# Embedding lookups, pairwise products and a small tower on one core: products by whole batches, lookups' high halves first, and the last block's first layer taken batch by batch

## The reference

```python
e = jnp.stack([tbl_f[ids[:, f]] for f in range(32)], axis=1)      # 512 x 32 x 256
z = jnp.einsum('bnd,bmd->bnm', e, e)[:, iu, ju]                    # 496 products i < j of each sample
h = jnp.concatenate([z, dense_ctx], axis=1)                        # 512 x 512
h = jnp.maximum(h @ W_top1 + b_top1, 0.0)                          # 512 x 512
h = jnp.maximum(h @ W_top2 + b_top2, 0.0)                          # 512 x 256
y = h @ W_top3                                                     # 512 x 1
```

## Time and profile before

| | |
|---|---|
| median of 3 runs | 164.88 us (163.91 to 168.86) |
| the profiled execution | 164.76 us, of which the span is 163.0 us |
| PE busy | 147.7 us, 91% of the span |
| PE weight loads | 132.3 us |
| DVE, ACT, POOL busy | 81.0, 78.3, 102.7 us |
| mean granted TensorE clock | 0.958 |

### The profile page before, as it was taken

How to read it: one execution, slowest core, us unless ns; L and a number is a source line. 1 busy time by engine, 2 the same in 40 slices (tenths; PEclk the granted TensorE clock), 3 DMA queues, 4 the chain that set the end, 5 groups by cost and what they waited for, 6 DMA issues and landing times.

```text
span 163.0 us, 6485 instructions
## 1 busy us (share of the span) xinstructions
PE 147.7 (91%) x2872; PEld 132.3 (81%) x2872; DVE 81.0 (50%) x212; ACT 78.3 (48%) x180; POOL 102.7 (63%) x110
## 2 busy tenths in 40 slices
PE   6996999999979969849985999999999999949994
PEld 6874888888878959839874989998898898949992
DVE  0798686766278597509500518207606605555000
ACT  3354848576686495607321723625426505363112
POOL 1677777777777777777777777777777777000000
PEclk9999999999999999965997899999999999986999
DMA  4899787868787889994443334333433343100000
GB/s 135 280 339 356 235 262 225 257 225 253 223 229 265 218 232 261 388 368 143 111 117 105 99 109 120 106 103 107 119 107 101 109 119 108 37 0 4 0 6 1
DMA packets 12926, 26.79 MB, mean 164 GB/s; under 512 B 3105, under 2 KB 3809, under 8 KB 12898
## 3 DMA queue, kind: packets, MB, share of 16 engines
q0 software_dynamic: 4992, 13.64, 29.3%
q1 hardware_dynamic: 7762, 12.47, 23.2%
q10 hardware_dynamic: 144, 0.26, 0.5%
HBM read 26.36 MB, written 0.00 MB: 162 GB/s over the span
## 4 chain that ended last, share of the span: by engine, by line
PE 81%; DMA 6%; issue 5%; ACT 4%; POOL 2%; DVE 0%
PE bank L505 24%; PE bank L553 16%; PE xt_ps L523 16%; PE bank L560 15%; PE bank L585 6%; DMA rows<-table,row_ids 4%; PE xt_ps L560 3%; ACT pairs L433 2%; DMA first_sb<-first_ids 2%; POOL rows L311 2%; PE bank L593 1%; ACT xt L416 1%; ACT high L403 1%; ACT kept L411 0%; DVE h L390 0%
## 5 line engine op out<-in xcount | busy, mean ns | idle before, releaser
L311 POOL DMA_INDIRECT rows<-table,row_ids x104 | 102.0, 981 | 34.8 <-issue 29.6
L416 ACT COPY xt<-xt_ps 128x512 f32<-128x512 f32 (+1 forms) x42 | 22.8, 559 | 45.1 <-PE xt_ps L523 44.8
L505 PE MATMUL bank<-one_hot,high 128*128 128x512 f32 (+1 forms) x128 | 35.2, 356 | 1.6 <-ACT kept L411 1.3
L553 PE MATMUL bank<-xt 128*32 128x32 f32 x2048 | 29.1, 203 | 8.3 <-issue 5.8
L553 PEld LDWEIGHTS bank<-xt 128*32 128x32 f32 x2048 | 24.0, 113 | 14.0 <-issue 8.5
L505 PE MATMUL bank<-one_hot,low 128*128 128x512 f32 (+1 forms) x128 | 33.5, 345 | 0.0
L342 DVE COPY xt<-xt_ps 128x512 f32<-128x512 f32 (+1 forms) x14 | 9.2, 654 | 44.4 <-PE xt_ps L523 44.4
L523 PE MATMUL xt_ps<-ident,rows 128*128 128x128 f32 x208 | 29.3, 290 | 1.5 <-DMA rows<-table,row_ids 1.5
L331 DVE TENSOR_SCALAR one_hot<-small_ids_sb,first_sb 128x512 fp32r<-128x512 int32 (+1 forms) x64 | 25.7, 427 | 7.8 <-PE bank L505 7.5
L523 PEld LDWEIGHTS xt_ps<-ident,rows 128*128 128x128 f32 x208 | 24.5, 147 | 3.8 <-DMA rows<-table,row_ids 2.0
L359 DVE COPY pairs<-bank 32x112 f32<-32x112 f32 (+3 forms) x88 | 23.5, 267 | 6.7 <-PE bank L553 5.7
(11 more groups left out here) (23 smaller groups left out, 39.6 us busy)
## 6 DMA issues: line engine op xcount, KB each, us to landing
small_sb<-small_tables SPq DMA_DIRECT2D x32, 256.0 KB, 4.3
w_sb<-w SPq DMA_DIRECT2D x8, 256.0 KB
rows<-table,row_ids POOLq DMA_INDIRECT x104, 3.8
small_ids_sb<-small_ids SPq DMA_DIRECT2D x3, 256.0 KB, 6.3
small_ids_sb<-small_ids SPq DMA_DIRECT2D x4, 128.0 KB, 4.3
w_sb<-w SPq DMA_DIRECT2D x1, 512.0 KB
small_ids_sb<-small_ids ACTq DMA_DIRECT2D x1, 256.0 KB, 3.5
ids_sb<-ids SPq DMA_DIRECT2D x1, 100.0 KB, 3.5
```

Source lines behind the costliest of these rows:

```text
L311: nc.gpsimd.indirect_dma_start(rows[:, i % ROWS, :], None, table, bass.IndirectOffsetOnAxis(ap=row_ids[:, i:i + 1], axis=0)).then_inc(gath ...
L416: nc.scalar.copy(*fill_parts(f)).then_inc(xt_act, 1)
L505: last = nc.tensor.matmul(banks[FOUND_BANKS[k][d]][:, of], part[:, k % TABLES, c, d * P:(d + 1) * P], one_hot[:, i % ONE_HOTS, of], start= ...
L553: done = nc.tensor.matmul(dots_ps[bank][Q * s:Q * (s + 1), u, g, :], x, x, start=(c == 0), stop=(c == DC - 1))
```

## The change

- `dots` are ordered by whole batches: each round has both halves of its batch in one run. The remaining 16 twos stand in rounds 0 to 3, two ahead of the batch and two behind it, instead of in rounds 0 to 5. Layer 1 of block 0 starts in round 5.
- `look_up` takes the four `high` products of its two chunks first, then the four `low` ones, and waits for `low` only there.
- The early fills come by threes (after twos 5, 8, 10, 12) and two after two 14. Warm-up has 9 products.
- A block's samples are numbered batch by batch, so that the 32 samples of a batch lie together in `pairs`. `b_top1` becomes a row of W1 against a row of ones in the dense part, so that a block's first relu is one ACT instruction of 128x512.
- In the last block layer 1 is turned round (`flip`): for each batch, 32 products with 32 samples as weights and 128 columns of W1 moving, four of them side by side in the four strips of PSUM partitions, accumulated over 8. The result (`flip_ps`) is copied to `flipped`, transposed by PE (`turn`), and copied with relu to `h1`. The last batch's six fetches are in four fills (2, 2, 1, 1). `h1` has two buffers.
- DVE moves three of the four strips of products from the second pair of batches on (before: two until the fourth pair), and only one of the first pair.

```diff
-WARM_UP = 12
+WARM_UP = 9
-FILLS_BEHIND = {2: (0, 1), 4: (2, 3), 6: (4, 5), 8: (6, 7), 10: (8, 9), 12: (10, 11), 14: (12, 13)}
+FILLS_BEHIND = {5: (0, 1, 2), 8: (3, 4, 5), 10: (6, 7, 8), 12: (9, 10, 11), 14: (12, 13)}
-LEAD_DOTS = [[0], [2], [4], [6], [8], [10], [13], [15], [17], [19], [21], [23], [25], [27, 28]]
-TRAIL_DOTS = [[1], [3], [5], [7], [9], [11, 12], [14], [16], [18], [20], [22], [24], [26], [29]]
+LEAD_DOTS = [[2 * n, 2 * n + 1] for n in range(6)] + [[2 * n, 2 * n + 1] for n in range(7, 15)]
+TRAIL_DOTS = [[]] * 5 + [[12, 13]] + [[]] * 8
-LEAD_TWOS = [3, 1, 2, 3, 2, 2] + [0] * (ROUNDS - 6)
-TRAIL_TWOS = [0, 2, 1, 0, 0, 0] + [0] * (ROUNDS - 6)
+LEAD_TWOS = [2, 2, 2, 2] + [0] * (ROUNDS - 4)
+TRAIL_TWOS = [2, 2, 2, 2] + [0] * (ROUNDS - 4)
-LAYER1_IN = {6: (0, [0, 1, 2, 3]), 7: (0, [4, 5, 6, 7]), 8: (1, [0, 1]), 9: (1, [2, 3, 4]),
+LAYER1_IN = {5: (0, [0, 1, 2]), 6: (0, [3, 4, 5]), 7: (0, [6, 7]), 8: (1, [0, 1]), 9: (1, [2, 3, 4]),
...
         def dve_quads(v):
-            return range(2 if v < 3 else 3)
+            return range(1 if v == 0 else 3)
...
             def look_up(two):
+                for part in (high, low):
+                    for i in range(2 * two, 2 * two + 2):
+                        if part is high:
+                            pe.wait_ge(one_hot_ready, i + 1)
+                        if i % 2 == 0:
+                            pe.wait_ge(high_ready if part is high else low_ready, two + 1)
...
+            def flip(m):
+                b = NB - 1
+                moved = UNIT * b + max(m, 1)
+                pe.wait_ge(moved_dve, moved)
+                pe.wait_ge(moved_act, moved)
...
+                for j in range(JJ):
+                    for q in range(QUADS):
+                        done = nc.tensor.matmul(flip_ps[m][Q * q:Q * (q + 1), :],
+                                                pairs[:, b % 2, j, m * SAMPLES:(m + 1) * SAMPLES],
+                                                w1_sb[:, j, q * P:(q + 1) * P], start=(j == 0), stop=(j == JJ - 1))
+                done.then_inc(flip_done, 1)
+            def turn(m):
...
+                nc.tensor.transpose(turn_ps[m], flipped[:, m, :], ident[:]).then_inc(turned, 1)
...
                 for f in fills_in(r):
+                    if f == NF - 2:
+                        flip(0)
+                        layer2_of(NB - 2)
+                        turn(0)
                     fill(f)
+            flip(1)
             for half in (2 * NM - 2, 2 * NM - 1):
                 dots(half)
-            layer2_of(b - 1)
...
+            flip(2)
+            flip(3)
+            layer3(NB - 2, l3_ps)
+            for m in range(1, BATCHES):
+                turn(m)
...
+            for n in range(N2):
+                for k in range(N1):
+                    layer2(NB - 1, n, k, last_l2_ps)
+            layer3(NB - 1, last_l3_ps)
```

More of the change, by code:

```diff
@@ L26 @@
 GATHERS = [(N_FIELDS - n) // PER_GATHER for n in LOOKED_UP]
-FILLS = [(n + 1) // 2 for n in GATHERS]
+FILLS = [[2] * (n // 2) + [1] * (n % 2) for n in GATHERS]
+LAST_FILLS = [2] * (GATHERS[1] // 2 - 1) + [1, 1]
 BLOCK = 128
@@ L62, with build_tower @@
 MOVES_IN = {2: 0, 4: 1, 6: 2, 7: 3, 9: 4, 11: 5, 13: 6}
-def build_tower(nc, table, first_ids, ids, small_tables, small_ids, dense, w1, b1, w2, b2, w3, out):
+def build_tower(nc, table, first_ids, ids, small_tables, small_ids, dense, w1, w2, b2, w3, out):
     D = table.shape[1]
@@ L76, in build_tower @@
     NG = sum(GATHERS) * HALF_BATCHES
-    NF = sum(FILLS) * HALF_BATCHES
+    NF = sum(len(fills) for fills in FILLS) * HALF_BATCHES + 1
     assert DC == 2 and KR == P and N_FIELDS == Q and NM == 2 * HALF_BATCHES
-    assert sum(TWOS_IN) == TWOS - FIRST_TWOS and NF == EARLY + ROUNDS * ROUND_FILLS
+    assert sum(TWOS_IN) == TWOS - FIRST_TWOS and NF == EARLY + ROUNDS * ROUND_FILLS + 1
     with ExitStack() as ctx:
@@ L132, in build_tower @@
         no_pairs_zeroed = sem("no_pairs_zeroed")
-        dense_in = sem("dense_in")
+        dense_in = [sem(f"dense_in{n}") for n in range(2)]
         weights_in = sem("weights_in")
@@ L162, in half_of, with fills_of @@
             return n // HALF_BATCHES
+        def fills_of(n):
+            return FILLS[half_of(n)] if n < NM - 1 else LAST_FILLS
         def first_fill(n):
-            return sum(FILLS[half_of(m)] for m in range(n))
+            return sum(len(fills_of(m)) for m in range(n))
         def batch_fill(f):
@@ L175, in fill_gathers @@
             n, u = batch_fill(f)
-            first = sum(GATHERS[half_of(m)] for m in range(n))
-            return range(first + 2 * u, first + min(2 * u + 2, GATHERS[half_of(n)]))
+            first = sum(GATHERS[half_of(m)] for m in range(n)) + sum(fills_of(n)[:u])
+            return range(first, first + fills_of(n)[u])
         def by_dve(f):
-            return f >= EARLY and f % 3 == 0
+            return f >= EARLY and f % 3 == 0 or f == NF - 1
         def moved_fills(f):
@@ L227, in fills_in @@
         def fills_in(r):
-            return range(EARLY + r * ROUND_FILLS, EARLY + (r + 1) * ROUND_FILLS)
+            return range(EARLY + r * ROUND_FILLS, EARLY + (r + 1) * ROUND_FILLS + (r == ROUNDS - 1))
         def dots_place(n):
@@ L492, in look_up @@
             def look_up(two):
-                for i in range(2 * two, 2 * two + 2):
-                    k, c = divmod(i, CHUNKS)
-                    pe.wait_ge(one_hot_ready, i + 1)
-                    if i % 2 == 0:
-                        pe.wait_ge(high_ready, two + 1)
-                        pe.wait_ge(low_ready, two + 1)
-                    of = looked_up_for(k)
-                    for part in (high, low):
+                k = 2 * two // CHUNKS
+                of = looked_up_for(k)
+                for part in (high, low):
+                    for i in range(2 * two, 2 * two + 2):
+                        c = i % CHUNKS
+                        if part is high:
+                            pe.wait_ge(one_hot_ready, i + 1)
+                        if i % 2 == 0:
+                            pe.wait_ge(high_ready if part is high else low_ready, two + 1)
                         for d in range(DC):
@@ L508, in look_up @@
                                 start=(c == 0 and part is high), stop=(c == CHUNKS - 1 and part is low))
-                    last.then_inc(chunk_used, 1)
+                        if part is low:
+                            last.then_inc(chunk_used, 1)
             def fill(f):
@@ L693 @@
     w1[0, 0:dense.shape[1], 0] = W1[len(iu):]
+    w1[0, dense.shape[1], 0] = a["b_top1"]
     arrays = {
@@ L700 @@
         "small_ids": ids_m[:, :, looked_up].reshape(B, most).T[None],
-        "dense": dense.T,
+        "dense": np.concatenate([dense.T, np.ones((1, B), dense.dtype)]),
         "w1": w1.reshape(P, JJ, H1),
-        "b1": a["b_top1"].reshape(-1, P).T,
         "w2": a["W_top2"].reshape(H1 // P, P, -1).transpose(1, 0, 2),
```

133 lines of the change are left out of this document (80 added, 53 removed).

## The result

The changed kernel takes 178.92 us (median of 4 runs, 174.76 to 182.56), the kernel before 164.39 (median of 4): ratio 1.072, 95% interval 1.052 to 1.093. It is slower. The ratio takes of each kernel only the runs within 1.5% of its fastest, so it is lower than that of the medians, 1.088. The profiled execution took 177.12 us with a span of 175.2, the one before 164.76 with 163.0, so 12.2 us of span are to be explained.

The account below looks back on a forecast made before the run. Two close bounds were taken: PE's own work and the fetches it follows. From 164.76 us, first tables -1.0, rounds -0.8 and the end -2.2 gave 160.8 us; the 8-in-10 range was 158.5 to 166.

Parts of the forecast that it names:

- The rounds, waits added: New PE waits in the rounds: +0.9 for `xt` ahead of batch 0, +0.3 in round 2, +6.6 code, +2.1 half clock.
- `kept` in round 2: In round 2 ACT's copy of the third table stands behind 12 product copies and four `high` casts: about +0.3 us.
- The same step, code: PE waits in the rounds for 256-instruction blocks of its program, more and shorter than before: +6.6 us (3 to 11).
- The price: Time a code block needs to come: about 5.2 us while tables load, 4.2 in the rest, 2.9 behind long products.
- Half clock: Loss in the rounds from the clock halving behind waits, taken as half of before: +2.1 us (0 to 5).
- Up to the end of the first tables: Start through the first four tables: fills by threes start earlier, but fetch 24 caps the gain; -1.0 us.
- The flips: Last block's turned layer 1, 64 matmuls of 128 columns each: four side by side, 1.8 us a flip.
- rival B: Flips less than four side by side, 2.25 to 2.9 us each: 162.6 to 165.2 us; chance 0.2, one by one 0.02.
- The end: From the end of round 13's layer 1 to the span's end: 22.0 us before, 19.8 now, -2.2.
- C: Slower: every round's run of 256 meets a block border and pays the full price: 172 us; chance 0.08.
- A: Code waits at low prices, no half clock, landings on time, PE held by fetches: 159.3 to 160.0 us; chance 0.2.
- D: Products' order gives nothing: code waits return at 9 to 10 us, half clock at 4: 164 us; chance 0.15.

## Why the prediction was wrong

**Step that failed: "The rounds, waits added."** It names three waits: `xt` ahead of batch 0, `kept` in round 2, and code. It has none for the fill that each whole batch reads. The profile of before had the row that shows the need, ACT's copies of fills at 559 ns each, and I asked only for batch 0 what stands between a copy and its product. Eight more batches have nothing there. Forecast 0, measured 5.3 us. I even booked the fills' new place (they "now follow layer 1 and not products") as a gain of 0.8.

```profile
L416 ACT COPY xt<-xt_ps 128x512 f32<-128x512 f32 (+1 forms) x42 | 22.8, 559 | 45.1 <-PE xt_ps L523 44.8
```

**The same step, code.** Forecast 6.6 us in eight places, by blocks that take 2.9 to 5.2 us from border to arrival. Measured in all 10.9 (8.0+2.1+0.8), of which 8.1 behind round 6's fills, where I had 1.0 (batches 8 and 11). Batch 3 came out as forecast (1.45 for 1.6), batches 0, 4 and 7 without a wait, batch 5 at half (0.54 for 1.1); batches 8, 9 and 12 waited 1.85, 1.94 and 2.18, where I had 0.3 for the first and nothing for the others, and the layers behind batches 11 and 14 waited 1.31 and 0.79, where I had 0.7 and nothing. The price was the wrong kind of number. A block's time from border to arrival isn't a property of the block: of the five in the quiet part, two had packets that started only 6.3 and 5.5 us behind their border. My working had slips too, of 0.5 us together: by the prices that I name, the terms of batches 3, 4, 5 and 8 are 1.7, 0.6, 1.3 and 0.6, and batch 7's 0.9 follows from none of them. That the blocks are of 256 and that the dense runs meet them was right: the waits in the quiet part end at PE records 3265, 3521, 4289, 4545 and 5313, all multiples of 256 apart.

**Half clock.** Forecast +2.1, as half of before. Measured were four stretches of 3.41 us, near waits of 1.45, 1.85, 1.94 and 2.05. Against the same instructions at full clock each cost about 1.6 us (lookups 1.05 for 0.64, layer 1 3.51 for 1.95), 6.5 together by this estimate. And none came behind the longest code wait, 2.18 at 137.92. The borderline I drew by the length of one stop, between 1.3 and 2.08, isn't there.

**Up to the end of the first tables, -1.0.** Measured +0.2 (fills at 41.23, before at 41.00). Fetch 20 made PE wait 1.80 at 37.30, and that took what fills by threes had won; I had only looked at fetch 24. In round 2 came another wait for rows, of 2.05, for which the forecast had nothing but 0.7 much later.

**Right.** The wait of 0.9 for `xt L424` (0.85). The flips: 64 matmuls in 1.88 us (156.65 to 158.53), against 1.8 forecast, so rival B is off and the estimate of 2.25 from the Trainium skill's "TensorE: Matmul & The Clock Gate" (Measured speedup vs the span model) is too long for them. The wait for code near flip 3 (0.83, forecast 0.7). No wait ahead of the last products. The end: counted as in the forecast, from the end of round 13's layer 1, it took 22.0 us before and 19.5 after, -2.5 against -2.2 forecast. From the start of the fills it is -1.8; the rest is the half batch that stood between that layer and the fills.

**Together.** Copies 5.3, code 4.3, half clock 4.4, the first tables 1.2 and the wait for rows in round 2 some 1.3 over their terms, less 0.3 each for `kept` and the end, make 15.9 of the 16.3 us by which the profiled execution missed 160.8.

**The rivals.** C came nearest (172) for a wrong reason: it put the loss on density, and density with the fills ahead costs nothing that can be measured (0.995). It had 0.08. A and D were both within the mechanism that fell. In the Trainium skill's "Runtime: NRT & Kernel Launch" (Instruction fetch mechanics) the fetch is hidden; neither trace agrees, with 5.8 us of waits for code before and 10.9 after.

## What to carry over

When work is merged into one longer run, ask of its first instruction what it reads and who wrote that last: two short runs with something between them hide a copy that one long run doesn't. A short wait ahead of a dense run can cost more than its length: here 4.7 us of such waits went, seven of the eight, and 13 us of time with them, since the code waits behind them went too. Moving producers ahead of other work only helps while their inputs are there: where PE had come close to the fetches, the fills that were put first waited 7.6 us for them.

## What the hardware showed that I had not expected

- A code packet (16 KB) takes 0.9 to 1.4 us in the changed kernel, and a PE that waits for it resumes 1.3 to 1.5 us after its end (109.76 to 111.22; 136.51 to 137.92), while tables load too (73.08 to 74.54). The rest of a block's time is the time until the packet starts.
- The granted clock went to half behind a stop of 1.45 us and not behind one of 2.18 in the same execution: the length of a single stop doesn't tell it.
- The same kernel took 165 us in some sets and 243 to 248 in others, on the same numbered chip too. The products of one kernel had 4 "issue" waits in one kind and 55 in the other, with 24 code packets in both kinds. A ratio from one kind says little on the other: 1.058 against 1.09 for the order alone, 0.94 against 1.00 for whole batches with the old front.
